# DLRM tower: a split first table, a twelfth lookup in the second pair of chunks, and lookups in the MLP's PSUM banks

## The reference

```python
e = jnp.stack([tbl_0[ids[:, 0]], ..., tbl_25[ids[:, 25]]], axis=1)   # (2048, 26, 128)
sd = jnp.einsum('bfd,bd->bf', e, dense)
ss = jnp.einsum('bfd,bgd->bfg', e, e)                                # upper triangle is kept
z = concatenate([dense, sd, pairs], axis=1)
h = concatenate([z, dense], axis=1)                                  # 607 columns
h = maximum(h @ W_top1 + b_top1, 0.0)                                # 512
h = maximum(h @ W_top2 + b_top2, 0.0)                                # 256
y = h @ W_top3
```

## Time and profile before

| | us |
|---|---|
| three runs | 361.7, 360.44, 361.55 (median 361.55) |
| the profiled execution | 359.05 |
| its span, first to last instruction | 357.1 |
| PE busy in the span | 335.2 |
| POOL busy | 241.8 |
| DVE busy | 206.6 |
| ACT busy | 204.0 |

### The profile page before, as it was taken

How to read it: one execution, slowest core, us unless ns; L and a number is a source line. 1 busy time by engine, 2 the same in 40 slices (tenths; PEclk the granted TensorE clock), 3 DMA queues, 4 the chain that set the end, 5 groups by cost and what they waited for, 6 DMA issues and landing times.

```text
span 357.1 us, 8260 instructions
## 1 busy us (share of the span) xinstructions
PE 335.2 (94%) x3388; PEld 286.4 (80%) x3388; DVE 206.6 (58%) x486; ACT 204.0 (57%) x267; POOL 241.8 (68%) x242
## 2 busy tenths in 40 slices
PE   0799999697999999999999999999999999999996
PEld 0677777586988888888998888898898888898885
DVE  0889898565328874628328886527427787145111
ACT  3378897484736575763663664872572666664111
POOL 6777777777777777777777777777777777720000
PEclk9999999999999999999999999999999999999999
DMA  6999729536355225254247243246236321124400
GB/s 154 241 261 250 194 61 269 148 93 164 76 143 138 65 69 132 55 127 124 53 108 183 75 105 84 68 95 155 59 83 177 100 64 48 51 51 121 113 24 1
DMA packets 46342, 40.93 MB, mean 115 GB/s; under 512 B 29039, under 2 KB 40423, under 8 KB 46306
## 3 DMA queue, kind: packets, MB, share of 16 engines
q1 hardware_dynamic: 38754, 24.94, 27.4%
q0 software_dynamic: 7552, 15.48, 17.3%
HBM read 34.64 MB, written 5.76 MB: 113 GB/s over the span
## 4 chain that ended last, share of the span: by engine, by line
PE 77%; POOL 8%; DMA 5%; issue 4%; DVE 3%; SPq 2%; ACT 1%; DVEq 0%
PE oh_ps L538 34%; PE dot_ps L556 15%; PE mlp_ps L574 15%; POOL rows L367 8%; PE mlp_ps L583 7%; PE tr_ps L522 7%; DMA rows<-tbl_dram,idx_sb 3%; DVE onehot L462 2%; DMA b_sb<-b_top_dram 2%; ACT feat L391 1%; DMA idx_sb<-idx_dram 0%; SPq L320 0%; SPq L316 0%; SPq L319 0%; DVE h L481 0%
## 5 line engine op out<-in xcount | busy, mean ns | idle before, releaser
L367 POOL DMA_INDIRECT rows<-tbl_dram,idx_sb x236 | 241.3, 1023 | 73.3 <-issue 70.7
L462 DVE TENSOR_SCALAR onehot<-ids_bc 125x512 fp32r<-125x512 int16 x360 | 142.4, 448 | 33.2 <-PE oh_ps L538 19.1
L538 PE MATMUL oh_ps<-onehot,table_hi 125*128 125x512 f32 x360 | 115.5, 402 | 12.0 <-DVE onehot L462 11.9
L538 PE MATMUL oh_ps<-onehot,table_lo 125*128 125x512 f32 x360 | 111.7, 392 | 0.0
L399 ACT ACTIVATE feat<-oh_ps 128x512 f32<-128x512 f32 x45 | 54.7, 1217 | 62.8 <-PE oh_ps L538 61.7
L391 ACT ACTIVATE feat<-tr_ps 128x512 f32<-128x512 f32 x59 | 73.0, 1241 | 26.3 <-PE tr_ps L522 25.8
L538 PEld LDWEIGHTS oh_ps<-onehot,table_hi 125*128 125x128 f32 x360 | 65.6, 190 | 24.4 <-issue 12.8
L538 PEld LDWEIGHTS oh_ps<-onehot,table_lo 125*128 125x128 f32 x360 | 68.1, 189 | 14.8
L556 PE MATMUL dot_ps<-feat 128*54 128x52 f32 x2048 | 57.8, 214 | 5.7 <-ACT feat L391 1.8
L556 PEld LDWEIGHTS dot_ps<-feat 128*54 128x54 f32 x2048 | 54.5, 130 | 10.1 <-issue 6.1
L471 DVE COPY dots<-dot_ps 54x416 f32<-54x416 f32 x56 | 33.2, 594 | 36.2 <-PE dot_ps L556 34.9
(11 more groups left out here) (24 smaller groups left out, 65.4 us busy)
## 6 DMA issues: line engine op xcount, KB each, us to landing
ids_bc<-ids_t_dram SPq DMA_DIRECT2D x45, 128.0 KB, 3.9
dots_scratch<-dots SPq DMA_DIRECT2D x28, 175.5 KB
rows<-tbl_dram,idx_sb POOLq DMA_INDIRECT x236
dots<-tbl_dram SPq DMA_DIRECT2D x6, 480.0 KB
w_sb<-tbl_dram SPq DMA_DIRECT2D x3, 480.0 KB
zt<-dots_scratch SPq DMA_DIRECT2D x12, 117.0 KB
dense_sb<-dense_f_dram SPq DMA_DIRECT2D x8, 128.0 KB, 2.6
zt<-tbl_dram SPq DMA_DIRECT2D x2, 480.0 KB
```

The lines of the kernel that those rows point to most:

```text
L367: nc.gpsimd.indirect_dma_start(rows[:, i % RING, k, t, :], None, tables[f], bass.IndirectOffsetOnAxis(ap=idx_sb[:, j % 2, x:x + 1], axis=0 ...
L462: last = nc.vector.tensor_scalar(onehot_part(m, part)[:, c, :], ids_bc[0:TP, m % IDSLOTS, :], float(part * PROWS + c), None, ALU.is_equal)
L538: last = nc.tensor.matmul(oh_ps[:, m % 2, :], table[0:TP, u, row * D:(row + 1) * D], onehot_part(m, part)[:, c, :], start=(table is table_ ...
```

## The change

1. **Start.** The raw first table comes in two halves of 512 columns, ahead of the other loads on SP; ACT and DVE split it by halves (`a0`, `b0`). The first ids are issued by ACT, and the ids of every lookup now lie in DRAM repeated for each of the 128 partitions. PE first does 24 transposes of the identity into `mlp_ps`.
2. **Second pair.** `LOOKUPS = (12, 12, 11, 11)`: a twelfth lookup instead of the odd unit of 4 gathers. Four lookups instead of two stand ahead of `d0`; the third and fourth (`EXTRA`) use the two `mlp_ps` banks. The first layer-1 step waits until both are copied out.
3. **Around it.** In `FIRST`, `r9` goes behind `l11`. The sum of the W_top1 blocks on DVE goes behind the first chunk's dot copies.
4. **End.** `r13` and `r14` of the last pair go to the tail as `q13` and `q14`, `k3` and `k4` go ahead of `d0`. Two of the last chunk's four dot stores are issued by ACT, and layer 3 of chunk 5 goes ahead of the last dot copies on DVE.

```diff
-LOOKUPS = (12, 11, 11, 11)
+LOOKUPS = (12, 12, 11, 11)
+EXTRA = (LOOKUPS[0] + 2, LOOKUPS[0] + 3)
...
-FIRST = ("i0 s0 i1 s1 l0 c0 ...
-         "l6 c6 s8 i8 r5 l7 c7 s9 i9 r6 f l8 c8 s10 i10 l9 c9 s11 i11 r8 l10 c10 r9 j0 l11 c11 e0 e1 e2 e3 r10 j1 "
+FIRST = ("i0 a0 b0 i1 s1 l0 c0 ...
+         "l6 c6 s8 i8 r5 l7 c7 s9 i9 r6 f l8 c8 s10 i10 l9 c9 s11 i11 r8 l10 c10 j0 l11 c11 r9 e0 e1 e2 e3 r10 j1 "
-SECOND = ("l0 q12 l1 q13 q14 d0 d1 d2 d3 d4 d5 d6 c0 d7 c1 o0 r0 o1 o2 r1 o3 r2 o4 "
+SECOND = ("l0 q12 l1 q13 l2 l3 q14 d0 d1 d2 d3 d4 d5 d6 c0 d7 c1 c2 c3 r0 o0 o1 o2 r1 o3 r2 o4 i6 "
...
-TAIL = "k2 d0 d1 d2 d3 d4 d5 d6 d7 k3 k4 o0 o1 o2 o3 o4 m0 m1 m2 m3 m4"
+TAIL = "k2 q13 k3 k4 q14 d0 d1 d2 d3 d4 d5 d6 d7 o0 o1 o2 o3 o4 m0 m1 m2 m3 m4"
...
+        def lookup_out(m):
+            if m in EXTRA:
+                return mlp_ps[:, EXTRA.index(m), :]
+            return oh_ps[:, m % 2, :]
...
-                sp.dma_start(ids_bc[:, m % IDSLOTS, :], ids_t[m:m + 1, :].broadcast_to([P, BOTH])
-                             ).then_inc(ids_loaded[m % IDSLOTS], DMA)
+                sp.dma_start(ids_bc[:, m % IDSLOTS, :], ids_t[m]).then_inc(ids_loaded[m % IDSLOTS], DMA)
...
+            def load_first_table():
+                for half in range(2):
+                    cs = slice(half * HALF, (half + 1) * HALF)
...
+            act.dma_start(ids_bc[:, 0, :], ids_t[0]).then_inc(ids_loaded[0], DMA)
...
+                    if kind == "d" and n == NCH and x == GUNITS - 1:
+                        act.wait_ge(dots_out_act, GUNITS * NCH)
+                        act.wait_ge(dots_out_dve, GUNITS * NCH)
+                        for q in range(Q // 2, Q):
+                            store_quarter(act, NCH - 1, q)
...
-            dve.wait_ge(weights_loaded, WEIGHT_DMAS * DMA)
-            nc.vector.tensor_tensor(w1_sb[:, ZC, :], w1_sb[:, ZC, :], w1_dense2, ALU.add).then_inc(w1_summed, 1)
...
                 dots_to_sbuf(n)
+                if j == 0:
+                    dve.wait_ge(weights_loaded, WEIGHT_DMAS * DMA)
+                    nc.vector.tensor_tensor(w1_sb[:, ZC, :], w1_sb[:, ZC, :], w1_dense2, ALU.add
...
                     if n == 0:
                         pe.wait_ge(weights_loaded, WEIGHT_DMAS * DMA)
                         pe.wait_ge(w1_summed, 1)
+                        pe.wait_ge(looked_up_out, EXTRA[-1] + 1)
...
+            pe.wait_ge(ident_made, 1)
+            for i in range(WARM):
+                last = nc.tensor.transpose(mlp_ps[:, i % 2, 0:P], ident[:], ident[:])
```

More of the change, by code:

```diff
@@ L86, in looked, with has_odd @@
     return sum(LOOKUPS[:j])
+def has_odd(j):
+    return LOOKUPS[j] == NO
 def unit_no(j, u):
-    return UNITS * j - (j > 0) + u - (j == 0 and u > ALONE)
+    return UNITS * j - sum(not has_odd(i) for i in range(j)) + u - (not has_odd(j) and u > ALONE)
 def pair(row):
@@ L238, in dot_copy, with store_quarter @@
             return dst, src
+        def store_quarter(engine, n, q):
+            products = dots_dram[n % 2, 0:NI * NJ, :].rearrange("(i j) b -> i j b", j=NJ)
+            row = TILE * (q // PACK) + NI * (q % PACK)
+            own = dots_of(n)[row:row + NI].rearrange("p (k j g) -> p k j g", k=PACK, j=NJ)
+            engine.dma_start(products[:, :, q * QS:(q + 1) * QS], own[:, q % PACK]
+                             ).then_inc(last_stored if n == NCH - 1 else dots_stored, DMA)
         block = ctx.enter_context(nc.Block())
@@ L274, in store_products @@
                 sp.wait_ge(dots_out_dve, GUNITS * (n + 1))
[L275 to L279, removed]
+                for q in range(Q if n < NCH - 1 else Q // 2):
+                    store_quarter(sp, n, q)
             def make_z(n):
@@ L298, in _ @@
             load_idx(0)
-            for u in range(IDSLOTS):
+            load_first_table()
+            for u in range(1, IDSLOTS):
                 load_ids(u)
@@ L330, in _ @@
                     make_z(n - 1)
-                    for u in range(NO - 2, NO):
+                    for u in range(NO - 2, LOOKUPS[j]):
                         load_ids(looked(j) + u)
@@ L355, in _ @@
             for j, u in itertools.product(range(NPAIR), range(UNITS)):
-                if j == 0 and u == ALONE:
+                if u == ALONE and not has_odd(j):
                     continue
@@ L374, in _, with split_first_hi @@
         def _(act):
+            def split_first_hi(half):
+                cs = slice(half * HALF, (half + 1) * HALF)
+                act.wait_ge(table_loaded[0] if half else half_loaded, 2 * DMA)
+                nc.scalar.activation(table_hi[0:TP, 0, cs], raw_table(0)[0:TP, cs], ACT.Copy
+                                     ).then_inc(hi_made if half else half_hi_made, 1)
             def split_hi(u):
@@ L483, in layer3 @@
                                                    ).then_inc(y_made, 1)
-            for u in range(NO + 1):
+            make_part(0, 0)
+            split_first_lo(0)
+            make_part(0, 1)
+            split_first_lo(1)
+            make_part(0, 2)
+            make_part(0, 3)
+            for u in range(1, NO + 1):
                 split_lo(u)
@@ L497, in _ @@
                     layer3(n - 2)
-                    for i in range(2 * PARTS + PLACES, NO * PARTS):
+                    for i in range(lead + PLACES, LOOKUPS[j] * PARTS):
                         make_part(looked(j) + i // PARTS, i % PARTS)
@@ L537, in lookup @@
                             row = part * PROWS + c
-                            last = nc.tensor.matmul(oh_ps[:, m % 2, :], table[0:TP, u, row * D:(row + 1) * D],
+                            last = nc.tensor.matmul(lookup_out(m), table[0:TP, u, row * D:(row + 1) * D],
                                                     onehot_part(m, part)[:, c, :],
```

70 lines of the change are left out of this document (53 added, 17 removed).

## The result

The changed kernel takes 369.23 us (median of four runs, 368.66 to 370.39), the kernel before 361.62 on the same chip: 1.0218 times as long, 95% interval 1.018 to 1.0255, +7.6 us where +5.7 was forecast. The profiled pair lies further apart: 370.39 against 359.05 us, +11.3, since one is the slowest of its runs and the other the fastest of its own.

The account below looks back on a forecast made before the run. Gathers were taken to bound the kernel until 42.6 us, with DMA engines full, and PE after that. The terms summed to +5.7 us on the 361.55 us median, giving 367.3 us, range 362.6 to 370.0.

Parts of the forecast that it names:

- Start, -0.4: Kernel start: first matmul comes sooner, but full DMA engines hold the gathers, so only 0.4 us is gained.
- r9 and the sum, -2.5: First pair: l11 starts sooner, 0.7 us gained; moving the weight sum removes the wait ahead of e2, 1.8 gained.
- Ahead of d0, -0.75: Second pair's last unit: ACT copies one unit there instead of two, with one transposition less behind; 0.75 us gained.
- Twelfth lookup, +3.2, and -0.25 for its gathers: Second pair: 16 more matmuls less 4 transposes lose 3.2 us; four gathers saved remove a 0.25 us wait.
- The MLP's banks, +4.3: Second pair, ahead of layer 1: o0 waits for ACT's fourth copy after d7; 4.3 us lost, the largest term.
- End, +2.1: Kernel end: d0 waits for ACT's copy, 1.3 us lost; stores and reloaded z cost 0.8 more.
- The 0.8 for stores and z: Tail: two store queues save 2.4 us of issue, yet short waits ahead of o2 and m0 lose 0.8 us.
- The rival in which z lands 13 us after d7 and m0 waits 2.7 us: Tail: four stores collide on the same 16 DMA engines; +8.1, 369.6 us; chance 0.11.
- the copies are hidden: Ahead of layer 1: ACT starts its copies before d7 ends, so o0 doesn't wait; +1.4, 362.95 us; chance 0.08.
- the early start carries through: First pair: gathers of units 4 and 5 land sooner, PE keeps its lead; +1.3, 362.9 us; chance 0.12.
- The gathers set the pace: Last unit of pair 1: POOL's gathers limit PE, so four fewer save 5 us; -3.6, 358 us; chance 0.06.

Follow-up runs that it names:

- the two small edits: Kernel before with only the ninth transpose step behind lookup l11 and the weight sum moved as in the change: 359.71 us, 0.996.
- old end: Changed kernel with the end of the kernel before: its order of last steps and on DVE, all four last stores on SP; 365.91 us, 1.013.
- stores on SP: Changed kernel in its own order to the end, but all four last stores on SP's queue, none on ACT's: 370.06 us, 1.024.
- fillers: Changed kernel with 36 unused operations put between r0 and the first layer 1, two runs: matmuls 373.05 us, 1.0324; transposes 368.29 us, 1.0182.
- filler matmuls: Changed kernel with 36 unused identity matmuls between r0 and the first layer 1: 373.05 us, 1.0324.

## Why the prediction was right in direction and short in size

- **Start, -0.4.** The lead was lost, as forecast: in the profiled pair the start gave 0.0 at r5, on the median 1.4 alone. Where it was lost was not all as forecast: PE waits 2.8 us for DVE's one-hots, and the 4.3 us for gathers stand ahead of r4 and two units before it, while the wait ahead of r5 is gone.
- **r9 and the sum, -2.5.** l0 of the second pair stands at 73.09, before at 75.56: -2.5. No wait is left ahead of e2. Alone it is worth 1.7, since gathers are late next; in the changed kernel l2 and l3 hide that of the last unit.
- **Ahead of d0, -0.75.** The wait is 1.27 instead of 1.84, and a transposition is saved. d0 stands at 90.26, forecast at 89.7.
- **Twelfth lookup, +3.2, and -0.25 for its gathers.** Measured 2.1, with an interval of 1.1 to 3.1.
- **The MLP's banks, +4.3.** The wait is 4.27 us, as worked out from ACT's copies. The step that failed in size stands behind it: that the matmuls after the wait cost what they cost before was assumed without being said. They took 2.6 us more.
- **End, +2.1.** Mis-sized: 3.3 us by the medians, 4.4 idle in the trace. The 0.8 for stores and z rested on 2.4 us saved by issuing on two queues, and that saving is none. The rival in which z lands 13 us after d7 and m0 waits 2.7 us had it nearly right, 13.7 and 2.24, but not for its reason: with all stores on SP, one after another, it is 12.9 us and 2.30.

In the profiled pair 5.6 us were missing: 2.6 for the clock, 2.3 for the end, 0.4 for the start and 0.38 for a gap in d7; about 5.7. The kernel before has a gap of 0.35 in its own tail, so this closes to about half a microsecond. On the medians, -1.4 - 1.7 + 2.1 - 0.75 + 4.3 + 2.6 + 3.3 = +8.5, against +7.6 measured; each measured term is uncertain by about 1 us. This sum adds the start and the small edits, which gave 1.7 together on the kernel before and not 3.1; with 1.7 it is +9.9. So it shows that no large term is missing, and not more.

That the forecast was only 1.9 us off on the median is in part luck: the clock (+2.6) and 1.2 of the end were missing, and 1.0 more from the start and perhaps some from the lookup's gathers took part of it back.

The rivals "the copies are hidden" and "the early start carries through" are refuted by the 4.27 us wait and by r5 at 42.57. "The gathers set the pace" is refuted for this change, but it isn't far off: with the two small edits alone PE waits 1.15 us at that very unit (162.12).

## What to carry to other kernels

A wait on the bottleneck engine is priced at its length and at the clock that it loses: look at the granted clock in and behind each wait, and behind two short ones close together (0.84 and 1.27 us cost 1.4 more here), and put work there that has to be done anyway. A step made sooner is worth only what the next late resource allows, so a gain is worked out together with that resource's own pace (here POOL's gathers); edits that cost something alone, like the lookups ahead of d0, can be what lets another gain through.

## What the runs showed of the hardware

- TensorE's granted clock fell from 1.00 to 0.50 within an idle wait (PE idle from 98.58, the clock 0.59 in the stretch from 101 to 102), after 55 us of nearly full work, and was back at 1.00 at 108, 5 us after work began again at 102.85. The price of about the same wait differed: the 24 matmuls behind it took 7.97, 7.88 (old end) and 7.11 us (stores on SP), against 5.35 to 5.43 without it. Ahead of m0, waits of 2.05 and 2.07 us cost 1.7 us behind them (fillers), waits of 2.24 and 2.30 none.
- Transposes counted for this clock. 36 of them held it at 1.00 (0.114 us each). At the start, 24 transposes took 4.84 us, 0.20 each, and the first lookup pair behind them took 0.70 us instead of the 1.19 in the earlier trace rows. The Trainium skill, "TensorE: Matmul & The Clock Gate", section "Part 4: PE-mode transpose", says that they don't count; these rows speak against it.
- That gain of a warm clock isn't safe: with the stores on SP, PE waited 2.92 us ahead of a lookup at 13.07, whose first pair then took 1.19 us; with the filler matmuls a wait of 3.37 us at the same place left it at 0.70.
